# Moving the fourth set of weight sums from the mixing stage to the h stage in the second group of a two-layer conditional FFN

## The reference, cut to what matters

```python
# layer 0
u = conv1d(x, w, groups=4, taps=9) + (cond @ c_weight.T)[:, :, None] + bias
x = x + u @ W.T + bias_f + lora(u)                 # W: 1024 x 1024
# layer 1
v = einsum('boi,bih->boh', mix_of_8(cond), x) + b  # a 64x64 matrix for each sample
scores = v @ Wr.T                                  # 64 experts of rank 16, the best 16 by softmax
h = v @ A.T                                        # A: 1024 x 1024 (64 experts x 16)
x = x + 2 * (h * gate) @ B.T                       # B: 1024 x 1024
```

## Time and profile before

| | |
|---|---|
| time, median of 3 runs | 657.62 us (656.94 to 659.66) |
| the profiled execution | 656.7 us, of which the span 654.9 us |
| PE busy | 648.1 us, 99% of the span |
| DVE, ACT, GpSimd busy | 451.4, 214.0, 73.8 us |
| PE clock granted | 0.999 of full speed |
| DMA | 157.98 MB, mean 241 GB/s; q1 62.7% and q10 4.8% of 16 engines' time |

### The profile page before, as it was taken

The page is one execution under the profiler, slowest core; times in us unless marked ns, Lnnn a source line. Parts: engine busy times, 40 slices in busy tenths (PEclk is TensorE's granted clock), DMA queues, the critical chain, the costliest instruction groups (busy, mean ns, idle before and its releaser), DMA issues.

```text
span 654.9 us, 8354 instructions
## 1 busy us (share of the span) xinstructions
PE 648.1 (99%) x3197; PEld 537.7 (82%) x3197; DVE 451.4 (69%) x690; ACT 214.0 (33%) x275; POOL 73.8 (11%) x91
## 2 busy tenths in 40 slices
PE   9999999999999999999999999999999999999997
PEld 8878888888897788888889788888879888888885
DVE  2859469549377788558769758636967856665785
ACT  2714135233144024335115312333423421433420
POOL 1598200000000160000000042000000000000000
PEclk9999999999999999999999999999999999999999
DMA  8587714986969926776976682287797664037795
GB/s 303 210 293 279 299 50 144 356 246 218 392 228 379 356 100 260 280 223 245 366 275 220 261 318 97 102 225 245 290 325 264 273 248 184 0 118 203 211 345 221
DMA packets 51594, 157.98 MB, mean 241 GB/s; under 512 B 5488, under 2 KB 6384, under 8 KB 51568
## 3 DMA queue, kind: packets, MB, share of 16 engines
q1 hardware_dynamic: 46240, 148.05, 62.7%
q10 hardware_dynamic: 5328, 9.61, 4.8%
HBM read 131.94 MB, written 25.71 MB: 241 GB/s over the span
## 4 chain that ended last, share of the span: by engine, by line
PE 91%; DVE 3%; DMA 3%; issue 1%; SPq 1%; ACT 0%; DVEq 0%
PE bank L1374 25%; PE bank L1376 24%; PE bank L1375 24%; PE bank L1388 9%; PE bank L1408 3%; DMA piece_lo<-kept 2%; PE bank L1395 2%; PE bank L1414 1%; PE bank L1402 1%; PE bank L1400 1%; PE bank L1415 1%; DVE x L925 1%; DMA gate<-hidden_w 1%; DVE u_lo L1012 1%; DVE work L932 1%
## 5 line engine op out<-in xcount | busy, mean ns | idle before, releaser
L893 DVE TENSOR_TENSOR piece_lo<-raw,piece_hi 128x1024 fp32r<-128x1024 f32 x60 | 74.1, 1239 | 90.0 <-ACT piece_hi L647 89.8
L647 ACT ACTIVATE piece_hi<-raw 128x1024 fp32r<-128x1024 f32 x60 | 63.4, 1058 | 147.1 <-PE bank L1376 103.2
L1374 PE MATMUL bank<-piece_hi,u_hi 128*128 128x512 f32 x272 | 107.9, 397 | 0.0
L1376 PE MATMUL bank<-piece_hi,u_lo 128*128 128x512 f32 x272 | 107.3, 395 | 0.0
L1375 PE MATMUL bank<-piece_lo,u_hi 128*128 128x512 f32 x272 | 107.3, 394 | 0.0
L1374 PE MATMUL bank<-v_hi,piece_hi 128*128 128x512 f32 x256 | 101.8, 398 | 0.0
L1376 PE MATMUL bank<-v_hi,piece_lo 128*128 128x512 f32 x256 | 101.1, 395 | 0.0
L1375 PE MATMUL bank<-v_lo,piece_hi 128*128 128x512 f32 x256 | 101.0, 394 | 0.0
L1374 PE MATMUL bank<-piece_hi,v_hi 128*128 128x512 f32 x192 | 76.0, 396 | 0.8 <-DMA piece_lo<-kept 0.8
L1376 PE MATMUL bank<-piece_hi,v_lo 128*128 128x512 f32 x192 | 75.8, 395 | 0.0
L1375 PE MATMUL bank<-piece_lo,v_hi 128*128 128x512 f32 x192 | 75.8, 395 | 0.0
(11 more groups left out here) (143 smaller groups left out, 800.7 us busy)
## 6 DMA issues: line engine op xcount, KB each, us to landing
raw<-pieces SPq DMA_DIRECT2D x76, 512.0 KB, 5.5
piece_hi<-kept SPq DMA_DIRECT2D x48, 512.0 KB, 4.7
piece_lo<-kept SPq DMA_DIRECT2D x48, 512.0 KB, 5.8
x<-x SPq DMA_DIRECT2D x16, 512.0 KB, 5.3
gate_x<-gates ACTq DMA_DIRECT2D x32, 256.0 KB
out<-x SPq DMA_DIRECT2D x32, 256.0 KB, 4.8
conv_in<-conv_x SPq DMA_DIRECT2D x15, 516.0 KB, 7.1
conv_in<-pieces SPq DMA_DIRECT2D x12, 512.0 KB, 8.8
```

The costliest lines, as they stand in the source:

```text
L647: act.activation(piece_hi[:, n % SLOTS, :], raw[:, r % RAWS, :], ACT.Copy).then_inc(s_piece_hi, 1)
L893: dve.tensor_tensor(piece_lo[:, n % SLOTS, :], raw[:, r % RAWS, :], piece_hi[:, n % SLOTS, :].bitcast(F32), ALU.subtract).then_inc(s_piece ...
L1374: pe.matmul(to, left_hi, right_hi, start=first, stop=False)
L1376: return pe.matmul(to, left_lo, right_hi, start=False, stop=last)
```

## The change

It touches the second group (g = 1) alone, in four places. The order of work on PE is not touched, nor what is computed.

- SP: the four `load_weights(3, i)` stand behind `fetch(6)` and `fetch(7)`, not ahead of them.
- ACT and DVE: the four `combined_hi(3)` and `combined_lo(3)` leave the mixing stage and stand together in the h stage, behind the splits of piece 18 and ahead of `gates_out` (ACT) and of the split of piece 19 (DVE).
- SP: the four `keep_weights(3)` stand ahead of `next_raw(18)` before; in the change two stand ahead of `next_raw(21)` (the eighth whole piece of the product with A) and two behind it.
- SP: the four `load_conv_in(g + 1)` of this group move from around `next_raw(18)` to behind `next_raw(23)`.

```diff
@@ SP, group(g, last)
                 next_raw(9)
+                fetch(g, 6)
+                fetch(g, 7)
                 if g == 1:
                     for i in range(4):
                         sp.wait_ge(s_comb_in[i], 48)
                         load_weights(3, i)
-                fetch(g, 6)
-                fetch(g, 7)
                 next_raw(14)
...
                 next_raw(16)
                 next_raw(17)
                 if g == 1:
-                    for step in range(4):
-                        keep_weights(3, step)
-                elif not last:
-                    load_conv_in(g + 1, 0)
-                    load_conv_in(g + 1, 1)
-                next_raw(18)
-                if g == 1:
-                    load_conv_in(g + 1, 0)
-                    load_conv_in(g + 1, 1)
-                if not last:
-                    load_conv_in(g + 1, 2)
-                    load_conv_in(g + 1, 3)
-                for n in range(19, 22):
-                    next_raw(n)
+                    for n in range(18, 21):
+                        next_raw(n)
+                    keep_weights(3, 0)
+                    keep_weights(3, 1)
+                    next_raw(21)
+                    keep_weights(3, 2)
+                    keep_weights(3, 3)
+                else:
+                    if not last:
+                        load_conv_in(g + 1, 0)
+                        load_conv_in(g + 1, 1)
+                    next_raw(18)
+                    if not last:
+                        load_conv_in(g + 1, 2)
+                        load_conv_in(g + 1, 3)
+                    for n in range(19, 22):
+                        next_raw(n)
                 if not last:
                     cond_bias(g)
                     mix_bias(g)
                 next_raw(22)
                 next_raw(23)
                 if g == 1:
+                    for t in range(4):
+                        load_conv_in(g + 1, t)
                     for i in range(4):
                         sp.wait_ge(s_comb[i], 32 * 4)
                 next_raw(26)
@@ ACT, group(g, last)
                 for i, c in enumerate(CHUNKS):
                     split_hi(g, MIX0 + i, v_hi[:, c, :], work[:, c, :])
-                    if g == 1 and i % 2 == 0:
-                        combined_hi(3, i // 2)
                 score_out(g, 5)
                 next_split(16)
                 gates_exp(g)
                 next_split(17)
                 next_split(18)
+                if g == 1:
+                    for step in range(4):
+                        combined_hi(3, step)
                 gates_out(g, 0)
@@ DVE, group(g, last)
                     if i:
                         mix_lo(g, i - 1, CHUNKS[i - 1])
-                    if g == 1 and i % 2:
-                        combined_lo(3, i // 2)
                 mix_lo(g, NCH - 1, CHUNKS[-1])
                 split_raw(g, 16)
                 choose(g, 1)
-                for n in range(17, 22):
+                split_raw(g, 17)
+                split_raw(g, 18)
+                if g == 1:
+                    for step in range(4):
+                        combined_lo(3, step)
+                for n in range(19, 22):
                     split_raw(g, n)
```

## The result

| | before | after |
|---|---|---|
| median of 6 runs | 657.26 us (655.57 to 659.66) | 673.71 us (672.67 to 675.27) |
| the profiled execution, its span | 656.7, 654.9 us | 675.27, 673.5 us |
| granted clock over the span | 0.999 | 0.989 |

The ratio is 1.0254, interval 1.0228 to 1.028: slower, by 16.4 us where 9.9 were forecast, and 0.7 us beyond the top of the range.

The account below looks back on a forecast made before the run. PE bounds the kernel, with 2.0 us to regain in the second group. Profiled execution 656.7 - 2.0 + 9.6 (h-stage stall) + 2.3 (clock) = 666.6 us; with 0.9 for the median, 667.5 us, range 659.5 to 673.

Parts of the forecast that it names:

- The load behind the fetches: W product, piece 6, second group: with the four weight loads behind it, PE's stall goes, gaining about 1.0 us.
- The stall at 247.04: Mixing stage, second group: PE waits 0.29 us for DVE's low part; moving the sums out gains 1.0 us there.
- The rival that the change does nothing: The stalls are not the loads' and sums' doing and nothing else moves: 657.6 us; chance 0.02.
- the price of a transfer: Queue q1: 512 KB transfers alone move 414 GB/s, so 1.27 us each.
- piece 22: h stage: lands at 296.6 against 287.7 before, behind the stores, so `winograd(22)` waits 3.5 us.
- the step headed "Piece 24": h stage: its low part lands at 313.5, due at 303.88: 9.6 us of stall in all, 6.1 ahead of `winograd(24)`.
- Low part 7 alone would hold `winograd(24)` until 310.3: h stage, DVE: low part 7 comes 13.7 us after piece 22's landing, and is due at 303.88.
- The queue packed tight: Rival, h stage: stores and loads fill all free moments, stall 5.3 us, 660.9 us; chance 0.12.
- the cover that holds: Rival, h stage: piece 22 lands by 290.2, costing nothing; the change is not slower, 655.6 us; chance 0.12.
- The backlog with the clock up: Rival, h stage: the same 9.6 us stall but the clock stays at full, 665.2 us; chance 0.20.
- All at the slow pace: Rival, h stage: every transfer at 2.36 us, stall 17.2 us, 675.1 us; chance 0.08.
- The clock: PE behind the 6.1 us stall ahead of `winograd(24)`: clock falls to 1.2 GHz, costing 2.3 us until it is back.

Follow-up runs that it names:

- the second of the better versions: The change with two sums right behind mixing, two behind the split of 18 with stores behind pieces 20 and 21, conv_in loads behind fetch(25): 659.03 us, ratio 1.0022.

## Why the prediction came out as it did

**Right: the sign, the places, and the first terms.** The load behind the fetches gives 0.95 us (1.0 forecast), and its cover held. The stall at 247.04 went, as forecast. The row at 244.46 did not: at 245.91 after the change PE still stands 0.24 us for DVE, so this one was not the sums' doing. In all the change gives 1.8 us, not 2.0. The rival that the change does nothing fell with it.

One reading under the price of a transfer was wrong. The earlier trace rows are not "512 KB transfers alone": in those 2 us q10 carried slices too, 72 of 262 packets.
```profile
q1 hardware_dynamic: 190, 0.68, 83.8%
q10 hardware_dynamic: 72, 0.15, 19.6%
```
The price of 1.27 us stands all the same. With the loads moved out of the h stage, q1 alone moves 412 GB/s at 304 to 306 us (0.82 MB in 2 us).

**Right in size, in part by luck: piece 22.** Eight transfers at 2.36 us and three at 1.27 gave a landing at 296.6; it was 295.9 on the same clock. The stall ahead of `winograd(22)` was 4.3 us, 3.5 forecast; in the run without slices 4 to 7 it is 3.56. But the term was all stores: with the same stores and the `conv_in` loads moved away, piece 22 lands 1.8 us earlier and the stall is 0.95 us. The loads behind piece 22, which the prediction left out of this term, have a share in it, and how they act is not shown. One sign was off: the transfer took 12.8 us from its issue, not "15 us or more". SP issued it as late as 283.78, since each issue took 1.2 to 1.5 us behind the stores and not the 0.3 to 0.4 of an empty queue.

**Wrong: the second stall, the step headed "Piece 24".** Forecast: `winograd(24)` 9.6 us late in all, by piece 24's fetch at 313.5. Measured: 16.4 us late, by low part 7, where low part 7 was forecast to be done at 310.3 and is done at 320.2 on the same clock. This one term holds the miss: 16.4 - 9.6 = 6.8 us, and the forecast was 6.2 too low. Two things in it failed:
- *The pace behind piece 22.* I took five transfers at 2.36 us and four at 1.27. The landing at 317.1 is 21.2 us behind 295.9 for nine transfers, 2.36 us each: all nine went at the first group's pace, since the slices were in flight through all of that time. By the fetch alone PE would have been 317.1 - 303.88 = 13.2 us late; this is 3.6 of the 6.8 us.
- *What the slices themselves do.* "Low part 7 alone would hold `winograd(24)` until 310.3" was the chain of the earlier trace rows set later by piece 22's delay, with DVE's own durations and no wait in it. I had counted the slices only as a drag on q1, and never q1 as a drag on the slices. In the change they land 4 to 5 us apart, low part 7 is done at 320.9 (320.2 on the clock of before), and this, not the fetch, ends the stall: the other 3.2 us. Each queue slows the other, as the runs without slices 4 to 7 and with the loads later show from both sides. The order of issue adds little to it. SP holds raw 27 and `fetch(24)` for the split of 23, and the fetch is issued at 305.23 instead of 294.94; but of these 10.3 us 0.7 are lag, 8.2 come from piece 22 and only 1.4 from a late slice (number 3), and a `conv_in` load (landed at 307.6) and raw 26 (at 310.8) are still in flight ahead of it.

The waits view of before, shown above, gave a hint: DVE waits 12.8 us for slices in 11 waits, of which 4.3 us in the first group's stretch and 2.0 in the second group's h stage. The stretch itself would have told it. By the semaphore records, the first group's slices 4 to 7 take 11.3 to 16.9 us to land there and land 4.0 to 5.6 us apart, as in the change. I read the earlier trace rows for q1's transfers and did not look at the slices beside them.

**The rivals.** The queue packed tight (660.9) and the cover that holds (655.6) are out: the latter needed piece 22 by 290.2. The former was also priced without the clock, though its stall of 5.3 us is longer than the 3 to 4 us of idleness that brought the clock down in the earlier trace rows. The backlog with the clock up (665.2) is out by the granted clock of 0.50 and 0.53. All at the slow pace (675.1) gave the nearest time, with a stall of 17.2 us; its pace was right behind piece 22, but the fetch, its bound, was not what held PE, so its nearness is in part luck.

**The clock.** Forecast 2.3 us, measured 1.7 behind the second stall. The forecast took its price from the first products of the kernel, but the windows view of that stretch (0 to 6 us) has the granted clock at 1.00, so those rows do not show what half clock costs. By the lag the price was 1.4 us with the loads moved out of the h stage, 2.3 without the stores, 2.4 with the loads alone, and 2.8 without slices 4 to 7, so 2.3 is a fair size. Short stalls cost as well: behind 2.10 us of idleness, in the second of the better versions, the granted clock is 0.50 from 306 to 308 us and the lag grows by 1.6. The first stall, 4.2 us idle, brought the clock to half too and cost 1.6 us, which I had said would hide ahead of the second; it lies inside the 16.4 above and cost nothing of its own, since low part 7 sets the end. The Trainium skill, "TensorE: Matmul & The Clock Gate", section on HAM oscillation, says that a kernel that waits long enough for a DMA resumes cold; the trace agrees, at 4.2 and at 10.3 us of idleness.

## What to carry to other kernels

A transfer that is moved costs more than its bytes where another engine's queue has loads in flight: price both queues, the one that it stands in and the one that it runs beside, and write down for each waiting instruction which of the two it waits for. Full use of the queue in the average (a share of 0.75) says little; take the pace from a stretch of the same kernel with the same mixture, for its whole length, and look there at both kinds of landing. Here 6 MB were moved into the stage with 1.9 us of slack, to gain 1.8 us.

## What was not expected of the hardware

- **How two queues share.** Packets of each queue in the changed kernel, 292 to 296 us (count, MB, share of 16 engines):
```profile
q1 hardware_dynamic: 273, 0.99, 85.2%
q10 hardware_dynamic: 110, 0.22, 18.8%
```
  q10 moves 0.22 MB in 4 us, so a slice of 0.26 MB takes 4.8 us, as long as DVE's items are apart. q10's packets are of 2.0 KB, q1's of 3.6 KB. The Trainium skill, "DMA: Bandwidth & Descriptors", section on queues, rings and completion order, says that a DMA engine takes turns between its queues packet by packet. The semaphore updates speak for 8 engines under a slice. If q1's packets are spread evenly, these 8 carry about half of them, 136 against 110 of q10: nearly turn for turn. The counts agree with that rule as far as this even division, which the profile does not show, holds.
- **Costs of transfers did not simply add.** 6.0 us for the stores, 8.7 or 10.7 us for the loads by two runs, 18.2 us for both; the excess lies between 1.5 and 3.5 us and is not known better.
- **The half clock does not cost the same each time.** 1.4 us by the lag behind a stall of 2.81 us, 2.8 behind one of 3.56, 1.7 behind the one of 10.31.
- **A small transfer suffers too.** The 128 KB store of the gates' table took 6.2 us to land, with the first stores of 512 KB on the other queue, against 2.6 before.
- **The convolution of the second group** differs by up to 2 us between profiled executions, with nothing changed there; one profiled pair can't show a gain of 1 us unless lags are compared stretch by stretch.
